# Expert layer: from products with all eight experts in every tile to tokens grouped by expert through lists in DRAM

## What is computed

```
x = x + attn(layernorm(x));  x = x + xattn(layernorm(x), ctx, mask);  x = x + ffn(layernorm(x))
def ffn(x, A, Bw, Wg):            # E = 8 experts, rank R = 64, D = 512
    prob = softmax(x @ Wg.T);  gate = argmax(prob);  prob_sel = prob[gate]
    h = einsum('nd,erd->ner', x, A) * one_hot(gate)[:, :, None]
    return einsum('ner,eor->no', h, Bw) * 4.0 * prob_sel
```

## Time and profile before

| | |
|---|---|
| median of 3 runs | 1554.63 us (1553.87 to 1555.09) |
| profiled execution, its own time | 1550.36 us |
| its span | 1548.2 us |
| busy: PE, DVE, ACT, POOL | 1405.0, 1098.3, 729.7, 756.4 us |
| mean granted TensorE clock | 0.966 of full speed |

### The profile page before, as it was taken

The page is one execution under the profiler, slowest core; times in us unless marked ns, Lnnn a source line. Parts: engine busy times, 40 slices in busy tenths (PEclk is TensorE's granted clock), DMA queues, the critical chain, the costliest instruction groups (busy, mean ns, idle before and its releaser), DMA issues. The chain is left out here.

```text
span 1548.2 us, 28131 instructions
## 1 busy us (share of the span) xinstructions
PE 1405.0 (91%) x10464; PEld 1150.8 (74%) x10464; DVE 1098.3 (71%) x2065; ACT 729.7 (47%) x1736; POOL 756.4 (49%) x573
## 2 busy tenths in 40 slices
PE   7887879999999989999996479999999999999998
PEld 5665767777777878777775368887888788878886
DVE  4345577777777787868764577878687878787865
ACT  5444567676676766666774232323232323232321
POOL 2321276867676776767676352423333433333310
PEclk9999989999999999999997689999999999999999
DMA  9999578888898988797888442222130303030000
GB/s 326 306 330 283 108 143 151 157 170 164 157 173 160 167 160 165 150 163 157 158 158 181 167 170 75 83 73 91 32 125 27 136 27 129 28 135 27 28 14 28
DMA packets 378998, 212.16 MB, mean 137 GB/s; under 512 B 337792, under 2 KB 337920, under 8 KB 375168
## 3 DMA queue, kind: packets, MB, share of 16 engines
q1 hardware_dynamic: 378880, 210.63, 56.3%
HBM read 76.37 MB, written 50.33 MB: 82 GB/s over the span
## 5 line engine op out<-in xcount | busy, mean ns | idle before, releaser
L622 POOL TENSOR_TENSOR shared<-a_probs,shared 128x768 f16<-128x768 f32 (+1 forms) x192 | 349.6, 1821 | 190.8 <-DVE shared L793 172.5
L691 ACT ACTIVATE a_probs<-a_score,a_neg_max 128x128 f32<-128x128 f32 (+3 forms) x512 | 264.7, 531 | 201.7 <-DVE a_neg_max L784 174.7
L784 DVE TENSOR_REDUCE a_neg_max<-a_score 128x2 f32<-128x256 f32 (+3 forms) x256 | 203.7, 817 | 108.3 <-PE a_score L910 107.7
L1184 POOL TENSOR_TENSOR b_probs<-b_probs,b_row_scale 128x1024 f32<-128x1024 f32 x32 | 61.2, 1912 | 175.3 <-DVE b_row_scale L1385 175.3
L936 PE MATMUL a_out_y<-a_v,a_turned 128*128 128x96 bf16 x1280 | 123.6, 212 | 19.9 <-DMA a_turned<-shared 11.8
L936 PEld LDWEIGHTS a_out_y<-a_v,a_turned 128*128 128x128 f16 x1280 | 99.7, 100 | 53.3 <-issue 35.3
L1154 POOL TENSOR_TENSOR b_rstd<-b_var,b_minus_half 128x1 f32<-128x1 f32 x64 | 35.2, 549 | 193.4 <-DVE b_var L1306 193.4
L1258 ACT ACTIVATE b_probs<-b_probs 128x1024 f32<-128x1024 f32 x32 | 33.9, 1059 | 196.4 <-DVE b_probs L1377 196.4
L937 PE MATMUL a_out_y<-a_v,a_turned 128*128 128x64 bf16 x1280 | 119.3, 196 | 0.0
L44 PE MATMUL a_gemm<-a_xt_hi,w_self_hi 128*128 128x512 f32 x256 | 110.3, 431 | 6.6 <-DVE a_yt_lo L758 4.7
L44 PE MATMUL b_score<-b_m_hi,b_xt_hi 128*128 128x512 f32 x256 | 105.4, 412 | 10.5 <-DVE b_m_lo L1341 6.9
(11 more groups left out here) (184 smaller groups left out, 3954.7 us busy)
## 6 DMA issues: line engine op xcount, KB each, us to landing
m_dram<-c_m_out SPq DMA_DIRECT2D x8, 2048.0 KB, 13.8
vw_dram<-shared SPq DMA_DIRECT2D x32, 512.0 KB, 8.3
shared<-m_dram SPq DMA_DIRECT2D x8, 2048.0 KB, 7.9
b_vw_raw<-vw_dram SPq DMA_DIRECT2D x8, 2048.0 KB, 7.8
c_w_raw<-w_group_dram SPq DMA_DIRECT2D x7, 1280.0 KB, 11.3
a_x_res<-x_dram SPq DMA_DIRECT2D x32, 256.0 KB, 3.5
x_dram<-a_x_res SPq DMA_DIRECT2D x32, 256.0 KB, 2.8
b_x<-x_dram SPq DMA_DIRECT2D x32, 256.0 KB, 2.7
```

The lines of the kernel that those rows point to most:

```text
L622: nc.gpsimd.tensor_tensor(part(u, 1), probs[:, u % PROB_SLOTS, 0:2 * columns_of(u // 2)], part(u, 0), ALU.subtract).then_inc(parts_ready, 1)
L691: ins = nc.scalar.activation(probs[:, u % PROB_SLOTS, to:to + width], score[:, j, at:at + width], ACT.Exp, bias=neg_max[:, c:c + 1], accum ...
L784: ins = nc.vector.tensor_reduce(neg_max[:, c:c + 2], score[:, 2 * half:2 * half + 2, at:at + width], AX, ALU.max, negate=True)
L1184: nc.gpsimd.tensor_tensor(probs[:, :, :], probs[:, :, :], row_scale[:, :].unsqueeze(2).to_broadcast([P, XH, S]), ALU.mult).then_inc(probs_ ...
```

## The change

In a tile's step `make_scores` comes first on TensorE and the mask addition first on VectorE; `probs` has two buffers. Expert products, their mask, transposes and output leave the tiles. What stays is the gate: logits of each tile, then once a batch `choose_experts` on VectorE (at t = 2 of the next batch) and `rank_tokens` (TensorE, 5 small matmuls) with `find_places` (VectorE) at t = 3, which give each token a place in the list of its expert; GpSimd writes 16 bytes a token to that place in DRAM with four indirect DMAs (`send_meta`). x2 goes to DRAM. The third layer norm becomes one small VectorE instruction (`shift`) and a ScalarE activation. On GpSimd the order of a step changes: scaling of probs and `deviation(3)` come ahead of `m_low` and `vw_low`.

Behind the tiles `experts()` reads the lists back and runs 39 tiles of 128 places, each with one expert: an indirect DMA gathers rows of x2, ScalarE normalises, TensorE transposes, multiplies with the chosen first matrix (8 matmuls of 128 or 64 columns) and second matrix (3 of 512), VectorE scales and adds, an indirect DMA scatters the rows to the output.

```diff
+                if done:
+                    _, dt_, n = done
+                    sp.wait_ge(x2_ready, n + 1)
+                    if ahead:
+                        load_x1(ahead)
+                    sp.dma_start(x2_dram[0:NOBODY, :].rearrange("(n p) c -> n p c", p=P)[bass.ds(n, 1)].rearrange("n p c -> p (n c)"),
+                                 x2[:, dt_, :]).then_inc(x2_stored[dt_], 16)
...
-            def deviation(k, n):
+            def deviation(k, n, to=None):
                 pool.wait_ge(var_ready[k], n + 1)
-                nc.gpsimd.tensor_tensor(ln[k][3][:, :], ln[k][2][:, :], minus_half[:, :], ALU.pow).then_inc(rstd_ready[k], 1)
+                nc.gpsimd.tensor_tensor(ln[2][3][:, :] if to is None else to, ln[k][2][:, :], minus_half[:, :], ALU.pow).then_inc(rstd_ready[k], 1)
...
+            def name_tokens(b, par):
+                if not (isinstance(b, int) and b == 0):
+                    pool.wait_ge(meta_sent, b * SENT)
+                    nc.gpsimd.tensor_tensor(meta[:, par, :, 0], meta[:, par, :, 0], two_batches[:, :], ALU.add).then_inc(tokens_named, 1)
...
+            def send_meta(b, par):
+                pool.wait_ge(place_ready, b + 1)
+                if isinstance(b, int) and b == 0:
+                    pool.wait_ge(meta_sent, SENT)
+                else:
+                    wait_all(pool, (tokens_named, b), (meta_sent, (b + 1) * SENT))
+                nc.gpsimd.tensor_tensor(pause[:, :], minus_half[:, :], minus_half[:, :], ALU.add)
+                for t in range(TT):
+                    nc.gpsimd.indirect_dma_start(meta_dram, bass.IndirectOffsetOnAxis(ap=place[:, t:t + 1], axis=0),
+                                                 meta[:, par, t, :], None).then_inc(meta_sent, 16)
...
             def step(b, t, par):
                 done, far = neighbour(b, t, -1), neighbour(b, t, 2)
                 new_vw = t == 0 and is_tile(b) and not (isinstance(b, int) and b == 0)
...
+                if is_tile(b):
+                    n = b * TT + t
+
+                    pool.wait_ge(scale_ready, n + 1)
+                    nc.gpsimd.tensor_tensor(probs[:, t % 2, :, :], probs[:, t % 2, :, :], row_scale[:, :].unsqueeze(2).to_broadcast([P, XH, S]),
+                                            ALU.mult).then_inc(probs_ready, 1)
+                if done:
+                    db, dt_, n = done
+                    dpar = parity(par, t, -1)
+                    if dt_ == 0:
+                        name_tokens(db, dpar)
+                    deviation(3, n, meta[:, dpar, dt_, 2:3])
                 if is_tile(b) and is_tile(b + 1):
                     for c in M_BESIDE[t]:
                         m_low(b + 1, c, 1 - par)
                 if new_vw:
-                    vw_low(b, 0)
-                if is_tile(b):
-                    n = b * TT + t
-
-                    pool.wait_ge(scale_ready, n + 1)
-                    nc.gpsimd.tensor_tensor(probs[:, :, :], probs[:, :, :], row_scale[:, :].unsqueeze(2).to_broadcast([P, XH, S]),
-                                            ALU.mult).then_inc(probs_ready, 1)
-                if done:
-                    deviation(3, done[2])
-                if new_vw:
-                    vw_low(b, 2)
-                    vw_low(b, 3)
+                    for c in VW_POOL:
+                        vw_low(b, c)
                 if isinstance(b, int) and b == 0 and t == 0:
-                    we_low(0)
-                    we_low(2)
+                    sorting_consts()
+                if t == 1 and isinstance(b, int) and b == 0:
+                    for k in range(4):
+                        nc.gpsimd.dma_start(meta_dram.rearrange("(k p a) c -> k p (a c)", k=4, p=P)[k], meta_fill[:, :]).then_inc(meta_sent, 16)
+                if t == 3 and not (isinstance(b, int) and b == 0):
+                    send_meta(b - 1, 1 - par)
...
+            def gather(j):
+                if j >= SLOTS:
+                    pool.wait_ge(slot_moved[j % SLOTS], j // SLOTS * 32)
+                nc.gpsimd.indirect_dma_start(gathered(j), None, x2_dram, bass.IndirectOffsetOnAxis(ap=tokens[:, j:j + 1], axis=0))\
+                    .then_inc(slot_moved[j % SLOTS], 16)
+
+            def experts():
+                send_meta(B - 1, (B - 1) % 2)
+                pool.wait_ge(block_ready, 1)
+                pool.wait_ge(meta_sent, (B + 1) * SENT)
+                nc.gpsimd.indirect_dma_start(meta_rows[0:TILES, :], None, meta_dram.rearrange("(q p) c -> q (p c)", p=P),
+                                             bass.IndirectOffsetOnAxis(ap=block_of[0:TILES, :], axis=0)).then_inc(meta_back, 16)
+                for t in range(TT):
...
+                for j in range(SLOTS - 2):
+                    gather(j)
+                for j in range(TILES):
+                    pool.wait_ge(x2_ready, SEEN + j + 1)
+                    nc.gpsimd.indirect_dma_start(out.rearrange("b t c -> (b t) c"), bass.IndirectOffsetOnAxis(ap=tokens[:, j:j + 1], axis=0),
+                                                 gathered(j), None, bounds_check=NOBODY - 1, oob_is_err=False).then_inc(slot_moved[j % SLOTS], 16)
+                    if j + SLOTS - 2 < TILES:
+                        gather(j + SLOTS - 2)
...
+                if turned:
+                    if not (isinstance(turned[2], int) and turned[2] == 0):
+                        act.wait_ge(gate_full, turned[2])
+                    copy_hi(flat(xt3_hi), turn[2][:, :], xt3_full, turned[2] + 1, xt3_hi_ready)
+                if ahead:
                     copy_hi(flat(xt2_hi), turn[0][:, :], xt2_full, ahead[2] + 1, xt2_hi_ready)
+                if here is not None:
+                    act.wait_ge(shifted, here + 1)
+                    nc.scalar.activation(probs[:, t % 2, :, :], probs[:, t % 2, :, :], ACT.Exp).then_inc(exp_ready, 1)
...
+                    for c in range(CHUNKS):
+                        split_vw(b, c)
+                if done:
+                    _, dt_, n = done
+                    dpar = parity(par, t, -1)
+                    act.wait_ge(shift_ready, n + 1)
+                    nc.scalar.activation(ln[3][4][:, :], x2[:, dt_, :], ACT.Identity, bias=meta[:, dpar, dt_, 3:4],
+                                         scale=meta[:, dpar, dt_, 2:3]).then_inc(xn_ready[3], 1)
...
+                nc.vector.tensor_reduce(logits[:, t, :], gate[:, 0:2 * E].rearrange("p (k e) -> p e k", k=2), AX, ALU.add)\
+                    .then_inc(logits_ready, 1)
...
             def step(b, t, par):
-                done, gated, made_tile, ahead, far = (neighbour(b, t, d) for d in (-1, -2, -3, 1, 2))
+                done, turned, gated, ahead, far = (neighbour(b, t, d) for d in (-1, -2, -3, 1, 2))
...
+                if here is not None:
+                    dve.wait_ge(score_full, here + 1)
+                    s = score[:, :, :].rearrange("p a (h s) -> p (a h) s", s=S)
+                    nc.vector.tensor_tensor(probs[:, t % 2, :, :], s, mask_add[:, bass.ds(b, 1), :].to_broadcast([P, XH, S]),
+                                            ALU.add).then_inc(masked, 1)
...
+                if here is not None:
+                    dve.wait_ge(masked, here + 1)
+                    nc.vector.tensor_reduce(row_max[:, :], probs[:, t % 2, :, :], AX, ALU.max).then_inc(max_ready, 1)
+                    dve.wait_ge(max_ready, here + 1)
+                    nc.vector.tensor_tensor(probs[:, t % 2, :, :], probs[:, t % 2, :, :], row_max[:, :].unsqueeze(2).to_broadcast([P, XH, S]),
+                                            ALU.subtract).then_inc(shifted, 1)
+                if turned:
+                    low(flat(xt3_lo), turn[2][:, :], flat(xt3_hi), xt3_hi_ready, turned[2] + 1, xt3_ready)
+                if ahead:
                     low(flat(xt2_lo), turn[0][:, :], flat(xt2_hi), xt2_hi_ready, ahead[2] + 1, xt2_ready)
...
-                if made_tile:
-                    low(flat(ht_lo), turn[1][:, :], flat(ht_hi), ht_hi_ready, made_tile[2] + 1, ht_ready)
-                if ahead and not start:
-                    low(flat(xt2_lo), turn[0][:, :], flat(xt2_hi), xt2_hi_ready, ahead[2] + 1, xt2_ready)
                 if far:
                     normalise(2, x1[:, far[1], :], far[2])
                 if done:
-                    normalise(3, x2[:, done[1], :], done[2])
+                    _, dt_, n = done
+                    dpar = parity(par, t, -1)
+                    dve.wait_ge(rstd_ready[3], n + 1)
+                    nc.vector.scalar_tensor_tensor(meta[:, dpar, dt_, 3:4], ln[3][1][:, 0:1], -1.0, meta[:, dpar, dt_, 2:3],
+                                                   ALU.mult, ALU.mult).then_inc(shift_ready, 1)
                 if t == 0 and here is not None and not start:
                     vw_low(b, VW_DVE[0])
...
+                    gb, gt, n = gated
+                    take_logits(n, gt)
+                    if gt == TT - 1:
+                        choose_experts(gb, parity(par, t, -3))
```

(86 more changed lines are left out.)

459 lines of the change are left out of this document (303 added, 156 removed).

## The result

The changed kernel takes 1665.85 us, median of four runs (1659.67 to 1667.86), against 1554.25 us: ratio 1.071, 95% interval 1.0685 to 1.0736, so slower by 7%. Its profiled span is 1657.9 us against 1548.2, 109.7 more. The forecast was 1602: the direction came, and 47 of the 111 us.

A forecast was written before the change was run, and what follows sets the result against it. TensorE was taken to bound the old loop (busy 549.17 of 559.35 us). Mask 31 at 1431 + 58 + 106 = 1595 against the span of 1548.2, +47, so 1554.63 + 47 = 1602 us; range 1575 to 1630.

The forecast's parts named there:

- The loop: 28 tiles in batches of four: steps of 19.6 + 18.0 + 14.8 + 19.0 = 71.4 us a batch, against 79.9 before.
- mask 31: Mask addition of tile 31, the last of the loop: forecast at 1431 us, against 1504.34 before.
- (a): At t = 0, scores wait for GpSimd's last `m_low`, behind probs' scaling and `deviation(3)`: step 19.6 us, not 13.5.
- (b): In every step, VectorE's small `shift` is held by GpSimd's next big instruction: 2.4 us taken, bounds 0 and 2.4.
- R1: Rival, faster: small VectorE instructions are not held in the loop; batch 63 us, total middle 1532; chance 0.22.
- R2: Rival: `shift` gets in ahead of GpSimd, `choose_experts` is held; 66.5 us a batch, 1568 in all; chance 0.20.
- The second hold at t = 0: At t = 0, one of three GpSimd `vw_low` holds VectorE another 2.4 us, in a step of 18.0.
- the small instructions of `choose_experts`: At t = 2, eleven VectorE instructions of 0.23 to 0.27 us add 2.75, in a step of about 19.0.
- the expert tile: 38 more tiles, each the largest of TensorE 2.1, VectorE about 1.9, GpSimd 2C = 2.8 us: 106 us.
- C: GpSimd's time for one indirect DMA, shown by no row: taken as 1.4 us, bounds 0.55 and 2.4.
- R3: Rival: TensorE falls to half clock after the loop's waits and in expert tiles (4.2 us each); 1685 us; chance 0.10.
- The way to the first tile: After mask 31, first tile and last scatter included: 44.1 + 7C = 53.9, plus 4.1 between: 58 us, against 43.86.

The follow-up runs named there:

- e1: Changed kernel with GpSimd's `m_low` alone put back ahead of the scaling of probs: 1621.94 us.
- e2: Changed kernel with `shift` worked out on ScalarE from a mean negated by VectorE, GpSimd's order left as changed: 1640.67 us.
- e4: As e3, plus one unread 512-column matmul in each expert tile ahead of its second product: 1681.85 us.
- e10: Changed kernel with gathers ahead of scatters, the waits ahead of the expert tiles filled, and three unread 512-column matmuls in each tile: 1613.14 us.
- e7: Changed kernel with GpSimd issuing the gather of tile j + 6 ahead of the scatter of tile j: 1666.4 us.
- e5: Changed kernel with the two waits ahead of the expert tiles filled and three unread 512-column matmuls in each tile: 1706.66 us.
- e6: As e5, but with six unread 512-column matmuls in each expert tile: 1658.83 us.
- e3: Changed kernel with 66 unread 384-column matmuls filling TensorE's two waits ahead of the expert tiles, tiles unchanged: 1668.64 us.
- e9: As e7, plus the waits ahead of the expert tiles filled and one unread 512-column matmul ahead of each product in each tile: 1638.57 us.
- e11: Changed kernel with the loop of e8 and the expert tiles of e10: 1554.55 us against 1554.79 for the kernel before, ratio 0.998.
- e12: e11 plus 14, 12 and 8 unread 512-column matmuls in the three last steps: 1551.62 us against 1556.49 for the kernel before, ratio 0.9963.
- e8: Changed kernel with `m_low` ahead of probs' scaling (second one of t = 2 behind `deviation(3)`) and `shift` on ScalarE: 1602.23 us.

## Why the prediction was right about the sign and wrong about the size

**The loop was right, by sum and by mechanism, but its steps were sized by luck.** Forecast 71.4 a batch and mask 31 at 1431; measured 70.6 in the mean (71.5 in the batch shown) and 1423.7. (a) stands: e1 took the wait away and 6.8 us a batch with it. But it was mis-sized: 24.0 instead of 19.6. The prediction forgot that `deviation(3)` itself waits for the weighted sum (the 1.83 us above), and left the half clock behind the pauses (8.0 us for 5.5 of scores) to a rival. (b) stands: 2.29 to 2.35 where 2.4 was taken, against a bound of 0, and e2 shows what it costs, 4.4 us a batch. The rule of the Trainium skill, "SBUF — State Buffer", section on who interferes with whom, names no size of the operands; the trace agrees with it, with 2.34 us for 128x1. R1 and R2 fall with that: `shift` never got in first. The second hold at t = 0, which was to make 18.0 us, did not come in the changed kernel (15.0; what is left of it is 0.85 us on the subtraction of t = 1), and the small instructions of `choose_experts` start 0.11 us apart instead of 0.23 to 0.27 (17.4 instead of 19.0). Errors of +4.4, -3.0, +0.3 and -1.6 cancelled.

**The step that failed is the expert tile, "each the largest of: TensorE ... 2.1; ... GpSimd a gather and a scatter, 2C = 2.8".** GpSimd's part was fair: 1.01 + 0.97 and 0.3 between, 2.6 a tile. TensorE's was counted at full clock, and it was 0.50 for all 39 tiles: 4.29 us instead of 2.8, 38 x 1.5 = 57 us of the 64 that are missing. Even at full clock it is an estimated 2.43, not 2.1. R3 described this, with 4.2 a tile, and got a chance of 0.10, for which the prediction gives no reason; its rows only showed a clock that had come back to 1.00 in the long loop. There, matmuls of 512 columns followed one behind the other; an expert tile has 13 of 64 and 128 columns and 3 of 512. The third window of the changed kernel shows TensorE busy for 163.01 of 163.01 us at 0.50: a busy engine, by the profile's count, is not yet one that gets its clock. That the clock is the cause, e4 shows within one execution (2.66 us a tile at 1.00, 4.86 at 0.50, the added matmul in both) and e10 over all tiles: with three wide matmuls more in each and the gathers ahead, 53 us less, though it does more work. Gathers ahead alone (e7) gave nothing, three matmuls alone (e5) cost 41 us, six alone (e6) held the clock. What it is in a mix of matmuls that lets the clock stay low, no run here isolates.

**The way to the first tile** was mis-sized too: 66.2 to the first output and 5.0 behind the last, 71.2 instead of 58. The prediction also added up its own list wrongly: the terms give 46.3 + 7C, not 44.1 + 7C, so 60.2 and not 58. The way ran at 0.67; the weighted sum of tile 31 alone takes 7.2 instead of 5.5 us, the fourth indirect DMA waited 2.88 us to be issued, and the first gathered tile needs 16.4 us from its gather to its output, where C + 2.7 + 7.0 = 11.1 was taken.

Together: 1602 - 7 (mask 31) + 13 (the way) + 57 (the tiles) = 1665, measured 1665.85. Of the 190.3 us lost behind mask 31, the clock in the tiles is an estimated 38 x (4.29 - 2.6) = 64, with GpSimd's 2.6 as the next bound; the rest is the price of the design: lists, gathers and 39 tiles behind the loop, where the old kernel hid most of its experts' products beside other work and needed 6.0 us a tile of TensorE.

## What to carry to other kernels

Before work is taken out of a full loop into a phase of its own, price that phase at both clock levels: here one of mostly narrow matmuls ran at half clock from end to end although the engine read as busy. When an operation moves on one engine's list, look for what the instruction behind it does to another engine: here a one-column VectorE instruction cost 2.3 us because of what GpSimd started next. And compare the end of the loop and the end of the kernel separately: the part up to the last mask addition gained 81 us here, and only the window behind it told where 190 went. Where an effect hangs on the clock, one execution of each version is not enough: 2 of 16 executions here fell back by 91 us.

## What the runs showed of the hardware that was not expected

- Half clock in a fully busy phase: 0.50 over 163.01 us with no gap in the rows of TensorE. Filling the waits ahead of it (e3) did not even keep 1.00 up to the first product. One 512-column matmul a tile kept 1.00 only until a wait of 2.12 us (e4), two until waits of 0.27 and 0.96 us (e9), three until one of 1.64 us (e5) or, with early gathers, to the end (e10, e11, e12), six to the end without early gathers (e6). In the loop it came back within 6 us of waits of 3.60 and 4.96 us. The Trainium skill, "TensorE: Matmul & The Clock Gate", section on a second failure mode, says that frequent short idle times between groups of matmuls can make the clock swing. These runs agree in part: short waits stood ahead of the falls in e3, e5 and e9, but the clock did not swing back (5.45 us a tile to the end of e5), e6 kept 1.00 with waits of 0.2 to 1.0 us in most tiles, and the changed kernel stayed at 0.50 with no idle time at all.
- A VectorE instruction can be held by several of GpSimd in a row: 8.51 us for one of 1.21, while three `vw_low` took 6.98 (e11, from 1147.35).
- An indirect DMA of 128 rows takes GpSimd mostly 0.95 to 1.06 us and 0.3 before the next, whether the rows have 16 bytes or 2 KB. But of the four sends at t = 3 one stood 5.9 to 7.2 us before it was issued, in every second batch (1025.46, 1167.62 and 1308.42 in the changed kernel). That cost the changed kernel nothing, since GpSimd still had to wait for the next `deviation`; in e8, e11 and e12 it had 0.2 us of slack or none, and the steps of 20 us above stand behind one of the three pauses of e11 and of e12, while e8 shows no such step; why, no run here settles.
